# Moving the third norm of the isolated rows from the second level of edge work to the fourth, and nine more dense units to the second level

## The reference

```python
x = _layernorm(x + L0(x, edges))                # MLP, then degree-normalised sums over edges
x = _layernorm(x + L1(x, edges, edge_weight))   # two weighted graph convolutions
x = _layernorm(x + L2(x, src, dst))             # attention over the edges of a node
x = _layernorm(x + L3(x, src, dst, edge_attr))  # MLP messages, summed, then an MLP per node
```

## Time and profile before

| | |
|---|---|
| median of 3 runs | 2968.99 us (2963.08, 2968.99, 2969.27) |
| the profiled execution | 2964.16 us; its span in the profile 2962.4 us |
| busy: TensorE / VectorE / ScalarE / GpSimd | 2167.5 / 1987.5 / 1436.1 / 2174.0 us |
| all 1600 gathers and scatters (`L860`, `L867`) | 2102 us busy |
| chain of waits | GpSimd 54%, issue 20%, VectorE 11%, TensorE 9% |
| DMA | 338.13 MB, mean 114 GB/s |

### The profile page before, as it was taken

How to read it: one execution, slowest core, us unless ns; L and a number is a source line. 1 busy time by engine, 2 the same in 40 slices (tenths; PEclk the granted TensorE clock), 3 DMA queues, 4 the chain that set the end, 5 groups by cost and what they waited for, 6 DMA issues and landing times.

```text
span 2962.4 us, 39045 instructions
## 1 busy us (share of the span) xinstructions
PE 2167.5 (73%) x10332; PEld 1145.4 (39%) x10332; DVE 1987.5 (67%) x3848; ACT 1436.1 (48%) x2755; POOL 2174.0 (73%) x1666
## 2 busy tenths in 40 slices
PE   3998999959878646766577768998355576666665
PEld 1444444434444323434344434444255333333332
DVE  5665688858888747788599985777599433333332
ACT  2876677746545335565345446676222232233232
POOL 7888877778887258888588858888333688888887
PEclk9999999979989868897799979999655687777777
DMA  7998522223666366767354443443387322222221
GB/s 212 277 280 232 140 58 59 56 55 82 138 136 133 93 132 153 164 150 164 84 115 115 114 100 84 99 109 80 80 189 187 84 57 55 56 56 57 56 50 25
DMA packets 624034, 338.13 MB, mean 114 GB/s; under 512 B 536607, under 2 KB 585101, under 8 KB 623818
## 3 DMA queue, kind: packets, MB, share of 16 engines
q1 hardware_dynamic: 550217, 288.96, 38.8%
q0 software_dynamic: 73600, 46.68, 9.3%
HBM read 203.61 MB, written 130.80 MB: 113 GB/s over the span
## 4 chain that ended last, share of the span: by engine, by line
POOL 54%; issue 20%; DVE 11%; PE 9%; DMA 3%; SPq 2%; ACT 1%; DVEq 0%; POOLq 0%; ACTq 0%
POOL g_row L860 38%; POOL x_with_info L867 8%; POOL out_rows L867 7%; PE bank L1078 2%; PE bank L1101 2%; DVE rT L1696 1%; PE pair L987 1%; DMA g_row<-t_x,gidx 1%; DVE agg L1718 1%; PE bank L987 1%; PE pair L1058 1%; DVE x_r L1673 1%; DVE agg L1776 1%; DVE ss L1619 1%; PE pair L1069 1%
## 5 line engine op out<-in xcount | busy, mean ns | idle before, releaser
L860 POOL DMA_INDIRECT g_row<-t_x,gidx x600 | 814.0, 1357 | 263.6 <-issue 218.9
L1288 ACT ACTIVATE hid<-pair,b_up 128x1000 f32<-128x1000 f32 x375 | 406.1, 1083 | 45.9 <-PE pair L1059 44.2
L1079 PE MATMUL bank<-hid,w_dn 128*64 128x500 f32 x750 | 423.6, 648 | 0.0
L1078 PE MATMUL bank<-hid,w_dn 128*64 128x500 f32 x750 | 423.6, 648 | 0.0
L860 POOL DMA_INDIRECT g_row<-x_with_info,src_i x200 | 275.4, 1377 | 69.3 <-issue 56.7
L1058 PE MATMUL pair<-xT,w_top 64*128 64x500 f32 x550 | 314.6, 653 | 13.0 <-ACT hid L1288 10.5
L860 POOL DMA_INDIRECT g_row<-t_h,gidx x200 | 260.4, 1302 | 81.1 <-issue 80.8
L1059 PE MATMUL pair<-xT,w_bot 64*128 64x500 f32 x550 | 315.0, 654 | 0.0
L860 POOL DMA_INDIRECT g_row<-in_x,dst_i x200 | 260.2, 1301 | 68.0 <-issue 67.6
L1269 ACT ACTIVATE xT<-bank 128x500 f32<-128x500 f32 x275 | 160.3, 583 | 280.2 <-DVE rT L1696 163.2
L867 POOL DMA_INDIRECT out_rows<-n_r,fidx x200 | 251.2, 1256 | 60.9 <-issue 60.6
(11 more groups left out here) (257 smaller groups left out, 5157.9 us busy)
## 6 DMA issues: line engine op xcount, KB each, us to landing
x_in<-in_x_cols SPq DMA_DIRECT2D x100, 250.0 KB, 3.2
x_with_info<-wide SPq DMA_DIRECT2D x50, 476.0 KB
wide<-in_x SPq DMA_DIRECT2D x50, 448.0 KB
out_rows<-x_r SPq DMA_DIRECT2D x100, 224.0 KB
l_k<-keep_row SPq DMA_DIRECT2D x150, 125.0 KB
l_a<-t_x SPq DMA_DIRECT2D x150, 112.0 KB
l_k<-on_row SPq DMA_DIRECT2D x50, 250.0 KB
t_x<-x_r SPq DMA_DIRECT2D x100, 112.0 KB
```

The costliest lines, as they stand in the source:

```text
L860: return g.indirect_dma_start(out=to, out_offset=None, in_=table, in_offset=bass.IndirectOffsetOnAxis(ap=index[:, tile:tile + 1], axis=0), ...
L1078: T.matmul(run.down[0:D, 0:CH], w_dn[a.stage][:, 0:D], hid[a.b2][:, 0, :], start=True, stop=True)
L1079: T.matmul(run.down[D:128, 0:CH], w_dn[a.stage][:, 0:D], hid[a.b2][:, 1, :], start=True, stop=True)\
L1288: A.activation(hid[a.b2][:, :, :], run.up[a.b2][:, :, 0:CH], ACT.Relu, bias=b_up[:, a.stage:a.stage + 1]).then_inc(Cn["hid"], 1)
```

## The change

Constants: DENSE_MIXED 3 to 0, BESIDE_B 22 to 31. The third norm's calls leave the slots of level B for those of level D on SyncE, ScalarE and VectorE; its stores are issued one slot later (2b+5), and SyncE runs the three slots that are left after level D's loop. VectorE's wait for the last third stores leaves the end of level B for the end of level D; SyncE waits for them too before level G's loads, which use the same tile `wide`.

```diff
--- before.py
+++ after.py
@@ -36,8 +36,8 @@
 EXT = 50
 EXT_EARLY = 8
 DENSE_FIRST = 49
-DENSE_MIXED = 3
-BESIDE_B, BESIDE_D, BESIDE_G = 22, 74, 0
+DENSE_MIXED = 0
+BESIDE_B, BESIDE_D, BESIDE_G = 31, 74, 0
 OWN_APART = 2
 
 
@@ -445,7 +445,7 @@
 
         def third_steps(k):
 
-            for step, at in (("rows", 4), ("st", 4), ("ld", 1), ("y", 0), ("sq", 1), ("ssum", 2), ("std", 3)):
+            for step, at in (("rows", 4), ("st", 5), ("ld", 1), ("y", 0), ("sq", 1), ("ssum", 2), ("std", 3)):
                 if (k - at) % 2 == 0 and 0 <= (k - at) // 2 < NI:
                     yield step, (k - at) // 2
 
@@ -765,7 +765,7 @@
             all_stored(sp, A_st, NI)
             level(lambda k, q: [(half(l_a[q]), rows_of(t1_d)[k]), (l_k[q][0:D, :], bc(keep_d, k, D)), (b_d1[q], bc(d1_d, k, D))],
                   B_ld, [LB["xb"]], B_st, LB["rows"], lambda k, q: (rows_of(t2_d)[k], v4(n_r[q][:, :])), behind=3,
-                  also=(B_bst, LB["base"], lambda k, q: (chunks(base_d)[k], v4(l_src[q][:, :]))), each=third, run=WITH_B)
+                  also=(B_bst, LB["base"], lambda k, q: (chunks(base_d)[k], v4(l_src[q][:, :]))), run=WITH_B)
 
             all_stored(sp, B_st)
             all_stored(sp, B_bst)
@@ -776,7 +776,9 @@
 
             all_stored(sp, C_st)
             level(lambda k, q: [(half(l_a[q]), rows_of(t3_d)[k])],
-                  D_ld, [LD["lky2"]], D_st, LD["zc"], lambda k, q: (z_d[k], zx[q % 2][:, :]), behind=2, run=WITH_D, late=1)
+                  D_ld, [LD["lky2"]], D_st, LD["zc"], lambda k, q: (z_d[k], zx[q % 2][:, :]), behind=2, run=WITH_D, late=1, each=third)
+            for k in range(NC + 2, NC + 5):
+                third(k)
             for r in range(2):
                 at_least(sp, D_st[r], 16 * len(range(r, NC, 2)))
             sp.dma_start(s1_c[:, 0, :], z_d[:, D, :]).then_inc(s_rows, 16)
@@ -786,6 +788,8 @@
             sp.dma_start(ex_d, s2_c[:, 1, :]).then_inc(s_rows, 16)
             sp.wait_ge(s_rows, 128)
             sp.wait_ge(s_ones, N_ONES)
+            for r in range(2):
+                sp.wait_ge(third_st[r], 32 * len(range(r, NI, 2)))
 
             def ld_sums(k):
                 q = k % 4
@@ -1377,7 +1381,7 @@
             at_least(act, LA["rows"], NI)
             all_stored(act, A_st, NI)
             act.wait_ge(s_idx, I_ALL)
-            shared_slots(slot_b, chain(WITH_B), WITH_B, 4, each=third)
+            shared_slots(slot_b, chain(WITH_B), WITH_B, 4)
 
             def after_c(at):
                 if c := at(4):
@@ -1408,7 +1412,7 @@
                         at_least(act, D_st[p], h * 32 + (q // 2) * 16)
                     A.activation(zx[p][:, :], AT[0:D + 2, 0:CH], ACT.Copy).then_inc(LD["zc"].sem, 1)
             at_least(act, LC["rows"], NC)
-            shared_slots(slot_d, chain(WITH_D), WITH_D, 4)
+            shared_slots(slot_d, chain(WITH_D), WITH_D, 4, each=third)
             act.wait_ge(LD["c"], D_EXP)
             A.activation(s2_c[:, :, :], s3_c[:, :, :], ACT.Exp).then_inc(LD["ca"], 1)
 
@@ -1846,9 +1850,7 @@
             at_least(dve, LA["rows"], NI)
             dve.wait_ge(s_idx, I_ALL)
             first, rest = chain(WITH_B)[1:]
-            shared_slots(slot_b, rest, WITH_B, 4, before=first, each=third)
-            for r in range(2):
-                dve.wait_ge([F["st0"], F["st1"]][r], 32 * len(range(r, NI, 2)))
+            shared_slots(slot_b, rest, WITH_B, 4, before=first)
             at_least(dve, LB["rows"], NC)
             all_stored(dve, B_st)
 
@@ -1910,7 +1912,9 @@
                     V.scalar_tensor_tensor(mv[:, :, D:128], half(l_a[q]), 0.2, half(l_a[q]),
                                            ALU.mult, ALU.max).then_inc(LD["lky2"].sem, 1)
             first, rest = chain(WITH_D)[1:]
-            shared_slots(slot_d, rest, WITH_D, 4, before=first)
+            shared_slots(slot_d, rest, WITH_D, 4, before=first, each=third)
+            for r in range(2):
+                dve.wait_ge([F["st0"], F["st1"]][r], 32 * len(range(r, NI, 2)))
 
 
             dc = [0]
```

## The result

The changed kernel takes 2945.8 us (median of 9 runs, 2937.2 to 2953.2) against 2966.5 for the kernel before (9 runs on the same chips, 2958.5 to 2977.4). The ratio of the two is 0.9926, 95% interval 0.9909 to 0.9943: 22 us faster, 17 to 27. The forecast was 2958 us, with 2944 to 2975 as its range: the measured time lies in it, 1.8 us from its fast end, and the gain is twice the 11 us forecast.

A forecast was written before the change was run, and what follows sets the result against it. GpSimd, the gathering engine, was taken to bound the kernel (54% of the chain). Terms -14 - 2.5 - 4.5 - 1 + 5.5 + 1 + 4.6 = -11 us, from the 2969.0 median to 2958 us; range 2944 to 2975.

The forecast's parts named there:

- level A: Level A with six real units less: no GpSimd buffer wait (5.2 us), last block turned sooner (9 us); -14, bounds -5 and -15.
- the ends of B: Level B's end without third blocks around its last chunk and without a third store among row stores: -4.5, bounds 0 and -6.4.
- D's end: Level D's end: constants wait for the last third store, +4.6 (+2 to +8); VectorE late at the last chunk, +1 (0 to +3).
- level C: Level C with three units less: GpSimd does not wait there, so only its end can gain; -1, bounds 0 and -3.
- the gathers of B: Level B's gathers, lengthened less without the third norm but more by nine added units: -2.5, bounds -5.5 and +1.
- with 34.6 gone a fifth of the 29 us goes: -6: Level B: third norm's two-input operations, 34.6 of some 160 us, leave; the 29 us of gather lengthening shrinks by 6.
- the gathers of D: Level D's gathers, lengthened by the third norm's two-input operations moved there: +5.5, bounds 0 and +23.
- I price the 34.6 us of two-input operations as in B, 0.18 us for each us: Level D: moved two-input operations lengthen gathers at B's rate, 29 / 160; +6, taken as +5.5.
- 1 (A stays late): Level A: an unmixed chain as slow as the gathers never catches up, the 9 us stay; result 2967 us, chance 0.15.
- 2 (B longer): Level B: with 30 units VectorE is late, the end keeps its 4.5 us, gathers lose 1; result 2966 us, chance 0.12.
- 3: Level D: VectorE becomes the bound, its 61.3 us of room exceeded, level ends 20 us later; result 2978 us, chance 0.15.
- 4, the port at its hardest: Level D: each gather is held for all of a two-input operation, 34.6 us instead of 5.5; result 2987 us, chance 0.06.

## Why the prediction was right or wrong

**Right, level A (-14; measured -15.3).** Both halves: no wait for a buffer, and the last block turned at once. With the mixed units back everything returned (430.7 us against 411.4). In the four further kernels with mixed units A's gathers and end took 429.6 to 432.0 us together, in the eight others without them 412.8 to 416.1, so the part is worth about 16.

**Right, the ends of B (-4.5; -5.3) and D (+4.6 and +1; +4.0).** For D's end the working held: a new wait for the last third stores, and constants that no longer hide. Half of the reason was wrong. I put 1 us down to VectorE's lateness, and with VectorE's part taken out the end did not get shorter. The size has some luck in it: in the five other kernels with the same steps there the end is 20.2 to 21.5 us, not 19.8.

**Right in size, its weight not seen, level C (-1; -1.8).** I costed three units less and took it for a free term. The runs show that C is where the change is decided: 52 units give an end of 21.3 to 22.2 us, 55 give 24.8 to 25.4, 61 give 35.5 and 40.4. The 31 units beside B, which the prediction treated as a cost, keep nine of those 61 out of C.

**Mis-sized, the gathers of B (-2.5, bounds -5.5 and +1; measured -8.7).** The step that failed is "with 34.6 gone a fifth of the 29 us goes: -6". Its cause holds: in levels A to D of the fourteen kernels 4746 gathers ran with no two-input operation beside them, and none of these was lengthened by over 0.1 us; the 6454 others were by 0.13 us on average. What failed is the price in proportion to the operations' length. Ten of the 200 gathers carry 11.7 of B's 30 us before, held through B's own operations, and with the third norm's arithmetic gone two or three do. Removing it from B gave 11.1 us (344.1 to 333.0) and 11.9 (to 332.2), of which its own second inputs were some 3.2. The other half, nine units more, was priced at +3.5 (-2.5 + 6) and gave some 2 (334.5 or 333.0 to 335.4).

**Mis-sized, the gathers of D (+5.5; measured +0.4).** The step is "I price the 34.6 us of two-input operations as in B, 0.18 us for each us". Kernels with and without the third norm's arithmetic in D differ by 2.2 us (324.0, 321.8), 0.06 for each us; the +0.4 has luck in it, because the kernel before is the longest of the six without. B's price has the long holds in it. D has none: no gather there is lengthened by over 0.63 us in any of the fourteen kernels.

The two misses fall to the same side. They make 11.3 of the 14.4 us by which the two profiled executions differ beyond the forecast, and put the total near the edge of the range.

**The rivals.** 1 (A stays late) and 2 (B longer) did not happen; GpSimd did not wait for VectorE in B. 3 is wrong for D, where room was left, but the same mechanism is real one level on the other side: with 31 units and the third norm VectorE, with its waits for TensorE, bounds B, and 36 units without the third norm cost 17 us. 4, the port at its hardest, is excluded: all of the third norm costs D's gathers 0.4 to 2.2 us.

## What to carry to other kernels

Where work is shared out beside a chain of levels, price the packing as a whole and not each move: here one part was worth -18, -1 or +2 us by what stood with it, since a unit that leaves one level enters another, and the level that is nearly full decides. The cheapest place for extra work is the engine's wait for data in the level with most of it (72.5 us in D held 56 us at a cost of 2), and it should end some chunks before the level does, so that neither its last stores nor its last rows stand in the end. And look at which gathers are long before pricing them by a mean: a few, held through operations in a row, can carry a third of it.

## What was not expected of the hardware

- A gather can be held through several two-input operations of VectorE in a row: 2.46 us in place of 1.27 with three, 1.75 where the second and third read one SBUF tile. Beside single-input operations alone no gather of levels A to D was lengthened by over 0.1 us, in any of the fourteen kernels.
- Level C's gathers got longer with fewer units beside them: 318.2 to 325.3 us with 52 or 55, but 327.4 with 47 and 327.0 with 46. VectorE waits more for gathers there (58.5 us over 45 waits with 47 units, 41.8 over 24 with 52). The added length lies on gathers with two-input operations beside them here too: 53 and 57 of the 200 are lengthened by over 60 ns, 35 in the changed kernel. No run was made on the cause.
- The third norm's own DMAs lengthened no gather that could be measured: 332.2 us in B with them (DMA share 0.74), 333.0 without (0.57).
